# One attention layer on TensorE: bodies of 512 tokens against bodies of 1024, with q and k in 512-column matmuls

## The chip, the core and the metric

The kernel runs on one core of a Trainium2 chip. The metric is the device time of one execution in microseconds: the median of 3 runs of the kernel before is 1513.44 us (1513.13 to 1513.64). The core's engines are named as the profile names them: PE (TensorE matmuls), PEld (its weight loads), DVE (VectorE), ACT (ScalarE), POOL (GpSimd) and SP (SyncE, which here only issues DMAs).

## What is computed

```
x: (2048, 64, 128) f32; W_query, W_key, W_value, W_res: (128, 128) f32; HEADS, ATT_D = 4, 32
q, k, v = heads(x @ W_query), heads(x @ W_key), heads(x @ W_value)    # each (head, 2048, 64, 32)
scores  = einsum('hbqd,hbkd->hbqk', q, k)                             # 64x64 per head and sequence
out     = softmax(scores, axis=-1) @ v                                # heads side by side again: 128 columns
y       = relu(out + x @ W_res)
```

2048 sequences of 64 tokens go through one attention layer of 4 heads, without scaling or mask. All is float32 at the borders. The projections are made from x and the weights split in two float32r parts each (hi and lo), as hi*hi + hi*lo + lo*hi, which is why each projection is three matmuls into one accumulation.

## The kernel before

A tile is 128 tokens, that is two sequences (`SEQS`) side by side. A body is `TILES` = 4 tiles, 512 tokens; there are N = 256 bodies. Every engine's program is written out by hand, with semaphores between the engines, in a function `step(i, n)` that works on several bodies at once, i and its neighbours. ACT, DVE, POOL and SP have all steps unrolled (`run`). PE has steps 0 to 3 and the last ones unrolled, and between them a loop whose lap is 4 steps (`run_looped`, `Fori(1, N // RING - 1)`: 62 laps).

What one body needs:

- DVE transposes x in 32x32 blocks and splits it (`split_x`: L349 x_t, L353 x_hi, L355 x_lo).
- PE projects q and k (`project_qk`, L196 to L198), half a body (256 tokens) a call: q into one half of the bank `ps_qk`, k into the other. ACT copies the bank into `qk` (L291).
- PE projects the values and the residual (`project_vr`, L209 to L211), half a body a call, into the bank `ps_vr`. ACT copies it into `vr` (L298). Each call waits until the copy before it has emptied its bank.
- PE forms the scores (`score`, L220), each head from 32 partitions, 32 calls a body, into columns 0 to 255 of the four banks of `ps_so`. DVE takes the row maximum (L364) and subtracts it (L369, `shifted`).
- PE transposes the shifted scores (`transpose_shifted`, L232), half a body a call, into the bank `ps_pt`; ACT takes the exponential into `probs_t` (L311).
- POOL spreads the values into block-diagonal form (L167, `v_diag`). PE multiplies probabilities and values (`weigh_values`, L241, 16 calls a body) into columns 256 and up (`O_AT`) of the same four banks of `ps_so`. A column of ones in the values gives the row sums.
- DVE takes the reciprocals of the sums and multiplies (L375, L379, `attn`), POOL adds the residual (L154, `y`), ACT clips at zero (L304), SP stores.

PE's order in step i is: scores of the first half of body i, values of body i-2, scores of the second half of body i, transposes of body i-1 (first half), q and k of body i+1 (first half), `project_vr` of body i (first half), then transposes, q and k, and `project_vr` of the second halves. The scores of body i wait for `shifted_ready` of body i-1 and `attn_ready` of body i-3, since all share the banks of `ps_so`. On the other engines the order is that of their `step` functions.

Each matmul in float32 with a tile of less than the whole array (L220, L241) leaves two records in the trace, so the 16 calls of one run of scores show as x32; L232 and the projections leave one record a call.

## Time and profile before

| | us |
|---|---|
| median of 3 runs | 1513.44 |
| profiled execution, whole | 1513.46 |
| its span, first to last instruction | 1511.7 |
| PE busy | 1493.1 |
| DVE busy | 1390.5 |
| ACT busy | 1044.5 |
| POOL busy | 872.2 |

The whole time of the profiled execution is 1.8 us over its span. A busy share counts an engine as busy while any of its instructions is under way. PE's matmuls overlap in its pipeline: each record is 0.2 to 0.3 us long, while the next one starts 0.007 to 0.12 us after it. For PE the distance from start to start is therefore what is to be read.

### The profile page before, as it was taken

The numbers are of one execution on the slowest core, as the hardware profiler recorded it, in microseconds if no ns is written. First come the engines' busy times: TensorE is split into PE (matmuls) and PEld (weight loads), VectorE is DVE, ScalarE is ACT, GpSimd is POOL, SyncE is SP. The second block draws the span as 40 slices with busy tenths as digits, with TensorE's granted clock in tenths as the row PEclk, the third lists the DMA queues.
The fourth block names the chain that finished last, engine by engine and source line by source line (L and its number), as shares of the span: only waits on it lengthen the run. The fifth ranks groups of instructions, "written<-read, shape, count | busy, mean of one in ns | idle before, by whom it ended". The sixth has DMA issues, their size and how long they took to land.

```text
span 1511.7 us, 77248 instructions
## 1 busy us (share of the span) xinstructions
PE 1493.1 (99%) x32768; PEld 1405.2 (93%) x32768; DVE 1390.5 (92%) x1793; ACT 1044.5 (69%) x1794; POOL 872.2 (58%) x1548
## 2 busy tenths in 40 slices
PE   7999999999999999999999999999999999999997
PEld 6999999999999999999999999999999999999997
DVE  6999999999999999999999999999999999999996
ACT  4677777777777777777777777777777777777775
POOL 3555555555555555555555555555555555555555
PEclk9999999999999999999999999999999999999999
DMA  3444444444444444444444444444444444444443
GB/s 59 98 85 96 85 96 86 96 86 95 86 96 85 96 85 96 85 96 85 96 86 96 86 96 85 96 86 95 86 96 85 96 85 96 85 96 85 96 86 77
DMA packets 677302, 135.36 MB, mean 90 GB/s; under 512 B 545888, under 2 KB 677216, under 8 KB 677216
## 3 DMA queue, kind: packets, MB, share of 16 engines
q1 hardware_dynamic: 675840, 134.30, 42.9%
q14 instruction: 74, 0.61, 0.1%
q10 hardware_dynamic: 1376, 0.26, 0.1%
q8 instruction: 12, 0.20, 0.1%
HBM read 67.37 MB, written 67.11 MB: 89 GB/s over the span
## 4 chain that ended last, share of the span: by engine, by line
PE 98%; issue 0%; POOL 0%; DVE 0%; ACTq 0%; DMA 0%; ACT 0%; POOLq 0%
PE ps_so L241 18%; PE ps_pt L232 17%; PE ps_so L220 14%; PE ps_qk L198 8%; PE ps_qk L196 8%; PE ps_vr L209 8%; PE ps_qk L197 8%; PE ps_vr L210 8%; PE ps_vr L211 8%; POOL y L154 0%; DMA w_raw<-in_L_rec_W_res_dram 0%; ACTq L334 0%; POOL v_diag L167 0%; DVE row_max L364 0%; ACTq L331 0%
## 5 line engine op out<-in xcount | busy, mean ns | idle before, releaser
L154 POOL TENSOR_TENSOR y<-attn,vr 128x256 f32<-128x256 f32 x512 | 387.4, 779 | 532.4 <-DVE attn L379 512.7
L167 POOL COPY v_diag<-vr 64x264 f32<-64x264 f32 x1024 | 478.7, 467 | 102.9 <-POOL y L154 39.9
L311 ACT ACTIVATE probs_t<-ps_pt 128x512 f32<-128x512 f32 x512 | 307.0, 600 | 160.2 <-PE ps_pt L232 160.1
L364 DVE TENSOR_REDUCE row_max<-ps_so 128x16 f32<-128x1024 f32 x256 | 313.5, 1225 | 69.7 <-PE ps_so L220 69.7
L298 ACT COPY vr<-ps_vr 128x512 f32<-128x512 f32 x512 | 300.6, 587 | 67.3 <-PE ps_vr L211 1.1
L196 PE MATMUL ps_qk<-x_hi,w_hi 128*128 128x256 f32 x1024 | 331.3, 323 | 10.5 <-DVE x_lo L355 9.7
L291 ACT COPY qk<-ps_qk 128x512 f32<-128x512 f32 x512 | 300.6, 587 | 56.6 <-PE ps_qk L198 9.0
L232 PE MATMUL ps_pt<-ident,shifted 128*128 128x128 f32 x2048 | 321.4, 280 | 0.8 <-ACT probs_t L311 0.8
L369 DVE TENSOR_TENSOR shifted<-ps_so,row_max 128x1024 f32<-128x1024 f32 x256 | 313.5, 1224 | 8.8
L241 PE MATMUL ps_so<-v_diag,probs_t 128*64 128x66 f32 x8192 | 296.2, 225 | 1.4 <-DVE attn L379 0.7
L198 PE MATMUL ps_qk<-x_lo,w_hi 128*128 128x256 f32 x1024 | 292.0, 285 | 0.0
L209 PE MATMUL ps_vr<-w_hi,x_hi 128*128 128x256 f32 x1024 | 290.7, 284 | 0.0
L210 PE MATMUL ps_vr<-w_lo,x_hi 128*128 128x256 f32 x1024 | 290.2, 283 | 0.0
L197 PE MATMUL ps_qk<-x_hi,w_lo 128*128 128x256 f32 x1024 | 290.0, 283 | 0.0
L211 PE MATMUL ps_vr<-w_hi,x_lo 128*128 128x256 f32 x1024 | 289.0, 282 | 0.0
L304 ACT ACTIVATE y<-y 128x512 f32<-128x512 f32 x256 | 161.5, 631 | 175.2 <-POOL y L154 175.2
L241 PEld LDWEIGHTS ps_so<-v_diag,probs_t 128*64 128x64 f32 x8192 | 260.6, 137 | 19.0 <-ACT probs_t L311 0.9
L355 DVE TENSOR_TENSOR x_lo<-x_t,x_hi 128x512 fp32r<-128x512 f32 x256 | 269.3, 1052 | 8.8
L220 PE MATMUL ps_so<-qk 32*64 32x64 f32 x16384 | 249.8, 230 | 0.0
L232 PEld LDWEIGHTS ps_pt<-ident,shifted 128*128 128x128 f32 x2048 | 225.7, 141 | 18.4 <-ACT probs_t L311 1.2
L220 PEld LDWEIGHTS ps_so<-qk 32*64 32x64 f32 x16384 | 179.2, 132 | 51.8 <-issue 0.2
L196 PEld LDWEIGHTS ps_qk<-x_hi,w_hi 128*128 128x128 f32 x1024 | 196.7, 192 | 10.9 <-issue 9.7
(20 smaller groups left out, 1527.2 us busy)
## 6 DMA issues: line engine op xcount, KB each, us to landing
x_in<-in_r_x_dram SPq DMA_DIRECT2D x1024, 64.0 KB, 2.2
out_dram<-y SPq DMA_DIRECT2D x256, 256.0 KB, 2.5
w_raw<-in_L_rec_W_query_dram ACTq DMA_DIRECT2D x1, 64.0 KB, 2.2
w_raw<-in_L_rec_W_key_dram ACTq DMA_DIRECT2D x1, 64.0 KB, 2.7
w_raw<-in_L_rec_W_value_dram ACTq DMA_DIRECT2D x2, 32.0 KB, 2.7
w_raw<-in_L_rec_W_res_dram ACTq DMA_DIRECT2D x2, 32.0 KB, 2.7
```

The source lines that it names most:

```text
L154: nc.gpsimd.tensor_tensor(y[:, n % 2, a * HALF:(a + 1) * HALF].rearrange("k t (p j d) -> k j (t p) d", j=2, d=D), attn[:, n % 2, a * HALF: ...
L167: nc.gpsimd.tensor_copy(v_diag[n % 2][j * F:(j + 1) * F, seq, :, :, :, j].rearrange("k a t p d -> k a (t p) d"), vr[n][seq * F:(seq + 1) * ...
L196: nc.tensor.matmul(ps, w_hi[:, w, :], x_hi[n][:, tok], start=True, stop=False)
L197: nc.tensor.matmul(ps, w_lo[:, w, :], x_hi[n][:, tok], start=False, stop=False)
L198: last = nc.tensor.matmul(ps, w_hi[:, w, :], x_lo[n][:, tok], start=False, stop=True)
L209: nc.tensor.matmul(ps, x_hi[n][:, tok], w_vr_hi, start=True, stop=False)
L210: nc.tensor.matmul(ps, x_hi[n][:, tok], w_vr_lo, start=False, stop=False)
L211: last = nc.tensor.matmul(ps, x_lo[n][:, tok], w_vr_hi, start=False, stop=True)
L220: last = nc.tensor.matmul(ps_so[s * F:(s + 1) * F, at:at + F], qk[rows, a, 0, b * F:(b + 1) * F], qk[rows, a, 1, b * F:(b + 1) * F], start ...
L232: last = nc.tensor.transpose(ps_pt[:, c * P:(c + 1) * P], pair, ident[:, :])
L241: last = nc.tensor.matmul(ps_so[s * F:(s + 1) * F, at:at + 2 * VW], probs_t[:, a, t * PAIRS + p, s * F:(s + 1) * F], v_diag[n % 2][:, s, a ...
L364: nc.vector.reduce_max(row_max[:, :].rearrange("q (h u) -> q h u", h=HEADS), scores, AX_X).then_inc(max_ready, 1)
```

## The change

A body becomes 8 tiles, 1024 tokens, in four `GROUPS` of two tiles; N falls to 128 bodies and PE's loop to 30 laps of 4 steps. The scores of a body fill all 512 columns of the four banks of `ps_so` (head h in bank h); the results of its values take the same banks later (group a in bank a), after the shifted scores have been read out of them. So scores and values of all bodies alternate on the four banks: scores of body i, then values of body i-1, each in one run. The values wait for `shifted_ready` of body i, the scores for `attn_ready` of body i-2. `project_qk` makes q or k alone, 512 tokens a call, in three matmuls of 512 columns that fill the bank `ps_qk`. `ps_pt` becomes two banks in turn, `ps_vr` stays one. DVE makes `x_lo` behind the reciprocal and the multiplication, POOL moves values in two parts around the residual, the clip comes one step earlier, and the instructions of DVE, POOL (L154) and ACT (L304) are twice as wide. Parts that only rename or widen are left out here:

```diff
-TILES = 4
+TILES = 8
 HALF = 2
+GROUPS = TILES // HALF
-HTOK = HALF * P
+GTOK = HALF * P
+QTOK = BANK
 VW = D + 1
-O_AT = TILES * F
...
-        qk = sb("qk", [P, 2, 2, HTOK])
-
-        vr = [sb(f"vr{n}", [P, 2, 4, HALF, PAIRS, VW]) for n in range(RING)]
-
-        v_diag = [sb(f"v_diag{n}", [P, SEQS, 2, HALF, PAIRS, 2, VW]) for n in range(2)]
+        qk = sb("qk", [P, 2, TOK])
+
+        vr = [sb(f"vr{n}", [P, 4, GROUPS, HALF, PAIRS, VW]) for n in range(RING)]
+        v_diag = [sb(f"v_diag{n}", [P, SEQS, GROUPS, HALF, PAIRS, 2, VW]) for n in range(2)]
-        probs_t = sb("probs_t", [P, 2, HALF * PAIRS, P])
+        probs_t = sb("probs_t", [P, GROUPS, HALF * PAIRS, P])
-        ps_qk, ps_vr, ps_pt = banks("ps_qk"), banks("ps_vr"), banks("ps_pt")
+        ps_qk, ps_vr = banks("ps_qk"), banks("ps_vr")
+        ps_pt = [banks(f"ps_pt{n}") for n in range(2)]
...
+                if m + g > 0 or has(i - 1):
+                    pe.wait_ge(qk_ready, upto(i, m * 2 + g) - 1)
+                tok = slice(g * QTOK, (g + 1) * QTOK)
+                nc.tensor.matmul(ps_qk[:, :], w_hi[:, m, :], x_hi[n][:, tok], start=True, stop=False)
+                nc.tensor.matmul(ps_qk[:, :], w_lo[:, m, :], x_hi[n][:, tok], start=False, stop=False)
+                nc.tensor.matmul(ps_qk[:, :], w_hi[:, m, :], x_lo[n][:, tok], start=False,
+                                 stop=True).then_inc(qk_done, 1)
...
-                    pe.wait_ge(vr_ready, halves(i, a) - 1)
+                if a > 0 or has(i - 1):
+                    pe.wait_ge(vr_ready, upto(i, a) - 1)
...
-            def score(i, a):
-                for u in range(a * HALF, (a + 1) * HALF):
+            def score(i):
+                for u in range(TILES):
                     for s in range(SEQS):
                         for h in range(HEADS):
-                            b = u % HALF * SEQS + s
                             rows, at = slice(h * D, (h + 1) * D), h * BANK + u * F
-                            last = nc.tensor.matmul(
-                                ps_so[s * F:(s + 1) * F, at:at + F], qk[rows, a, 0, b * F:(b + 1) * F],
-                                qk[rows, a, 1, b * F:(b + 1) * F], start=True, stop=True)
-                return last
+                            tok = slice((u * SEQS + s) * F, (u * SEQS + s + 1) * F)
+                            last = nc.tensor.matmul(ps_so[s * F:(s + 1) * F, at:at + F], qk[rows, 0, tok],
+                                                    qk[rows, 1, tok], start=True, stop=True)
+                last.then_inc(s_done, 1)
...
-                if a == 1 or has(i - 1):
-                    pe.wait_ge(pt_ready, halves(i, a) - 1)
+                if a >= 2 or has(i - 1):
+                    pe.wait_ge(pt_ready, upto(i, a) - 2)
...
-                        last = nc.tensor.transpose(ps_pt[:, c * P:(c + 1) * P], pair, ident[:, :])
+                        last = nc.tensor.transpose(ps_pt[a % 2][:, c * P:(c + 1) * P], pair, ident[:, :])
...
-                for a in range(2):
+                for a in range(GROUPS):
...
-                                at = (a * HALF + t) * BANK + O_AT + p * 2 * VW
+                                at = a * BANK + (t * PAIRS + p) * 2 * VW
...
             def step(i, n):
                 if has(i):
+                    if has(i - 2):
+                        pe.wait_ge(attn_ready, i - 1)
                     if has(i - 1):
                         pe.wait_ge(shifted_ready, i)
-                    if has(i - 3):
-                        pe.wait_ge(attn_ready, i - 2)
-                    pe.wait_ge(qk_ready, halves(i, 0))
-                    score(i, 0)
-                if has(i - 2):
-                    pe.wait_ge(pt_ready, halves(i - 2, 1))
-                    pe.wait_ge(v_moved, (i - 2) * 4 + 4)
-                    if not has(i):
-                        pe.wait_ge(shifted_ready, N)
-                        pe.wait_ge(attn_ready, i - 2)
-                    weigh_values(i - 2, n)
-                if has(i):
-                    pe.wait_ge(qk_ready, halves(i, 1))
-                    score(i, 1).then_inc(s_done, 1)
-                if has(i - 1):
-                    pe.wait_ge(shifted_ready, i)
+                    pe.wait_ge(qk_ready, upto(i, 3))
+                    score(i)
+                else:
+                    pe.wait_ge(shifted_ready, N)
+                    pe.wait_ge(attn_ready, i - 1)
+                if has(i - 1):
                     transpose_shifted(i - 1, n + 1, 0)
                 if has(i + 1):
-                    project_qk(i + 1, (n + 1) % RING, 0)
+                    project_qk(i + 1, (n + 1) % RING, 0, 0)
+                if has(i - 1):
+                    transpose_shifted(i - 1, n + 1, 1)
                 if has(i):
                     project_vr(i, n, 0)
                 if has(i - 1):
-                    transpose_shifted(i - 1, n + 1, 1)
-                if has(i + 1):
-                    project_qk(i + 1, (n + 1) % RING, 1)
+                    transpose_shifted(i - 1, n + 1, 2)
+                if has(i + 1):
+                    project_qk(i + 1, (n + 1) % RING, 0, 1)
+                if has(i - 1):
+                    transpose_shifted(i - 1, n + 1, 3)
                 if has(i):
                     project_vr(i, n, 1)
+                if has(i + 1):
+                    project_qk(i + 1, (n + 1) % RING, 1, 0)
+                if has(i - 1):
+                    pe.wait_ge(v_moved, (i - 1) * 8 + 8)
+                    if has(i):
+                        pe.wait_ge(shifted_ready, i + 1)
+                    pe.wait_ge(pt_ready, upto(i - 1, 3))
+                    weigh_values(i - 1, n + 1)
+                if has(i + 1):
+                    project_qk(i + 1, (n + 1) % RING, 1, 1)
+                if has(i):
+                    project_vr(i, n, 2)
+                    project_vr(i, n, 3)
...
-                act.wait_ge(qk_done, halves(i, a))
+            def copy_qk(i, m, g):
+                act.wait_ge(qk_done, upto(i, m * 2 + g))
...
-                nc.scalar.copy(qk[:, a].rearrange("p w t -> p (w t)"), ps_qk[:, :]).then_inc(qk_ready, 1)
+                nc.scalar.copy(qk[:, m, g * QTOK:(g + 1) * QTOK], ps_qk[:, :]).then_inc(qk_ready, 1)
...
             def step(i, n):
-                if has(i - 3):
-                    clip(i - 3, (n + 1) % 2)
                 if has(i - 1):
                     exp_pt(i - 1, 0)
                 if has(i + 1):
-                    copy_qk(i + 1, 0)
+                    copy_qk(i + 1, 0, 0)
+                if has(i - 1):
+                    exp_pt(i - 1, 1)
                 if has(i):
                     copy_vr(i, n, 0)
                 if has(i - 1):
-                    exp_pt(i - 1, 1)
-                if has(i + 1):
-                    copy_qk(i + 1, 1)
+                    exp_pt(i - 1, 2)
+                if has(i + 1):
+                    copy_qk(i + 1, 0, 1)
+                if has(i - 1):
+                    exp_pt(i - 1, 3)
                 if has(i):
                     copy_vr(i, n, 1)
+                if has(i + 1):
+                    copy_qk(i + 1, 1, 0)
+                if has(i - 2):
+                    clip(i - 2, n)
+                if has(i + 1):
+                    copy_qk(i + 1, 1, 1)
+                if has(i):
+                    copy_vr(i, n, 2)
+                    copy_vr(i, n, 3)
...
-            def split_x(i, n):
+            def transpose_x(i, n):
...
+
+            def rest_of_x(i, n):
                 dve.wait_ge(xhi_ready, i + 1)
                 nc.vector.tensor_tensor(x_lo[n][:, :], x_t[:, :], x_hi[n][:, :].bitcast(F32),
                                         ALU.subtract).then_inc(xlo_ready, 1)
...
+                if has(i):
+                    shift_scores(i, n)
                 if has(i + 2):
-                    split_x(i + 2, (n + 2) % RING)
+                    transpose_x(i + 2, (n + 2) % RING)
+                if has(i - 1):
+                    normalize(i - 1, n + 1)
+                if has(i + 2):
+                    rest_of_x(i + 2, (n + 2) % RING)
```

The order on PE, first around the scores. Before, two runs of scores (`ps_so<-qk`) with the values (`ps_so<-v_diag`) between them, then the transposes (`ps_pt`):

```order
L220 MATMUL ps_so<-qk 64x64 x16
L241 MATMUL ps_so<-v_diag,probs_t 64x66 x16
L220 MATMUL ps_so<-qk 64x64 x16
L232 MATMUL ps_pt<-ident,shifted 128x128 x4
L196 MATMUL ps_qk<-x_hi,w_hi 128x256
```

And in the changed kernel, where line numbers are its own:

```order
L225 MATMUL ps_so<-qk 64x64 x64
L236 MATMUL ps_pt<-ident,shifted 128x128 x4
L201 MATMUL ps_qk<-x_hi,w_hi 128x512
L202 MATMUL ps_qk<-x_hi,w_lo 128x512
L203 MATMUL ps_qk<-x_lo,w_hi 128x512
L236 MATMUL ps_pt<-ident,shifted 128x128 x4
```

The scores of 8 tiles stand in one row of 64 calls, and the values have moved out from between them, to stand behind the third block of q and k.

The order on PE at the end of a step, with what each instruction waits for. Before, the second `project_vr` stands behind q and k, and its predecessor on the same bank is a whole group of q, k and transposes away:

```order
L232 MATMUL ps_pt<-ident,shifted 128x128 x3
L196 MATMUL ps_qk<-x_hi,w_hi 128x256 [waits qk_ready,xlo_ready]
L197 MATMUL ps_qk<-x_hi,w_lo 128x256
L198 MATMUL ps_qk<-x_lo,w_hi 128x256
L196 MATMUL ps_qk<-x_hi,w_hi 128x256
L197 MATMUL ps_qk<-x_hi,w_lo 128x256
L198 MATMUL ps_qk<-x_lo,w_hi 128x256
L209 MATMUL ps_vr<-w_hi,x_hi 128x256 [waits vr_ready]
```

And in the changed kernel, the third and the fourth `project_vr` of a body (the start of each is the row with a wait):

```order
L214 MATMUL ps_vr<-w_hi,x_hi 128x256 [waits vr_ready]
L215 MATMUL ps_vr<-w_lo,x_hi 128x256
L216 MATMUL ps_vr<-w_hi,x_lo 128x256
L214 MATMUL ps_vr<-w_hi,x_hi 128x256
L215 MATMUL ps_vr<-w_lo,x_hi 128x256
L216 MATMUL ps_vr<-w_hi,x_lo 128x256
L214 MATMUL ps_vr<-w_hi,x_hi 128x256 [waits vr_ready]
L215 MATMUL ps_vr<-w_lo,x_hi 128x256
```

The fourth `project_vr` stands right behind the third, on the same bank, with nothing between them.

## Rows read from the trace of the kernel before

**Rows 1.** Page, part 1: busy time, share of the span, instructions

```profile
span 1511.7 us, 77248 instructions
PE 1493.1 (99%) x32768; PEld 1405.2 (93%) x32768; DVE 1390.5 (92%) x1793; ACT 1044.5 (69%) x1794; POOL 872.2 (58%) x1548
```

**Rows 2.** Windows view, first values product to the last laps: busy, PEclk, DMA share, GB/s

```profile
24.80:1500.80 1476.00, 1475.27 (x32480) 1389.27 (x32469) 1376.11 (x1773) 1032.95 (x1776) 858.88 (x1523) 1.00 0.43 90
```

**Rows 3.** Timeline of a steady body: start us, us, engine, line, tiles, shapes, count

```profile
803.05 0.28 PE L210 MATMUL ps_vr<-w_lo,x_hi 128*128 128x256 f32 x1
803.17 0.28 PE L211 MATMUL ps_vr<-w_hi,x_lo 128*128 128x256 f32 x1
803.38 0.49 PE L220 MATMUL ps_so<-qk 32*64 32x64 f32 x32
803.79 1.16 PE L241 MATMUL ps_so<-v_diag,probs_t 128*64 128x66 f32 x32
804.88 0.49 PE L220 MATMUL ps_so<-qk 32*64 32x64 f32 x32
805.30 0.66 PE L232 MATMUL ps_pt<-ident,shifted 128*128 128x128 f32 x4
805.49 1.23 DVE L364 TENSOR_REDUCE row_max<-ps_so 128x16 f32<-128x1024 f32 x1 [0.25 <-PE ps_so L220]
805.71 0.36 PE L196 MATMUL ps_qk<-x_hi,w_hi 128*128 128x256 f32 x1
805.91 0.28 PE L197 MATMUL ps_qk<-x_hi,w_lo 128*128 128x256 f32 x1
807.23 0.60 PE L232 MATMUL ps_pt<-ident,shifted 128*128 128x128 f32 x4
807.58 0.36 PE L196 MATMUL ps_qk<-x_hi,w_hi 128*128 128x256 f32 x1
807.78 0.28 PE L197 MATMUL ps_qk<-x_hi,w_lo 128*128 128x256 f32 x1
809.19 0.49 PE L220 MATMUL ps_so<-qk 32*64 32x64 f32 x32
```

**Rows 4.** One line's view (L220), same body: duration ns min/median/max, first and last start

```profile
L220 PE MATMUL ps_so<-qk x64: 217/217/266, 803.4 to 805.2; 32*64 32x64 f32 x64
```

**Rows 5.** Timeline at the start of the execution, PE

```profile
12.16 0.55 PE L196 MATMUL ps_qk<-x_hi,w_hi 128*128 128x256 f32 x1 [0.83 <-ACT qk L291]
12.72 0.41 PE L198 MATMUL ps_qk<-x_lo,w_hi 128*128 128x256 f32 x1
12.93 0.41 PE L196 MATMUL ps_qk<-x_hi,w_hi 128*128 128x256 f32 x1
19.66 0.91 PE L220 MATMUL ps_so<-qk 32*64 32x64 f32 x64
```

**Rows 6.** Timeline at the end of the execution: a PE matmul that waited for ACT

```profile
1498.50 0.58 ACT L298 COPY vr<-ps_vr 128x512 f32<-128x512 f32 x1
1499.13 0.39 PE L209 MATMUL ps_vr<-w_hi,x_hi 128*128 128x256 f32 x1
1499.36 0.28 PE L210 MATMUL ps_vr<-w_lo,x_hi 128*128 128x256 f32 x1
1499.83 0.28 PE L211 MATMUL ps_vr<-w_hi,x_lo 128*128 128x256 f32 x1
1500.15 0.58 ACT L298 COPY vr<-ps_vr 128x512 f32<-128x512 f32 x1 [0.42 <-PE ps_vr L211]
```

**Rows 7.** Groups by line: count, busy us, mean ns, idle before and releaser

```profile
L167 POOL COPY v_diag<-vr 64x264 f32<-64x264 f32 x1024 | 478.7, 467 | 102.9 <-POOL y L154 39.9 <-ACT vr L298 16.4 <-PE ps_so L241 0.2
L369 DVE TENSOR_TENSOR shifted<-ps_so,row_max 128x1024 f32<-128x1024 f32 x256 | 313.5, 1224 | 8.8
L379 DVE TENSOR_TENSOR attn<-ps_so,inv_sum 128x512 f32<-128x512 f32 x256 | 177.1, 692 | 8.8
L298 ACT COPY vr<-ps_vr 128x512 f32<-128x512 f32 x512 | 300.6, 587 | 67.3 <-PE ps_vr L211 1.1
```

**Rows 8.** Page, part 6: a load's time from issue to landing

```profile
x_in<-in_r_x_dram SPq DMA_DIRECT2D x1024, 64.0 KB, 2.2
```

More of the change, by code:

```diff
@@ L97, in run @@
         def run(step):
-            for i in range(N + 3):
+            for i in range(N + 2):
                 step(i, i % RING)
@@ L107, in run_looped @@
                     step(ring * RING + n, n)
-            for i in range(N - RING, N + 2):
+            for i in range(N - RING, N + 1):
                 step(i, i % RING)
@@ L113, in has, with upto @@
             return not isinstance(i, int) or 0 <= i < N
+        def upto(i, g):
+            return i * GROUPS + g + 1
         def halves(i, a):
@@ L338, in _ @@
             act.wait_ge(ones_ready, 1)
-            copy_qk(0, 0)
-            copy_qk(0, 1)
+            for m in range(2):
+                for g in range(2):
+                    copy_qk(0, m, g)
             run(step)
```

145 lines of the change are left out of this document (72 added, 73 removed).

## The prediction

> **What bounds the kernel now.** I read the busy times first: PE 1493.1 of 1511.7 us, DVE 92%, ACT 69%, POOL 58% [rows 1]. The windows view over the 1476 us in which the bodies repeat has PE busy for 1475.27 us [rows 2]: PE waits for nobody there, so the time is the sum of PE's own starts. That window also has all 61 lap ends of PE's loop in it, so jumping back costs PE nothing visible today. The timeline of one body says what the sum is made of, read from start to start [rows 3]. The body lasts from 803.38 to 809.19, 5.81 us, so 11.62 us for 8 tiles and 256 x 5.81 = 1487 us of the span; the other 24 us are the filling and the emptying of the pipeline. Within a body:
>
> - A projection matmul of 256 columns starts 0.12 after the one before (803.05, 803.17).
> - Into the scores it is 0.21 (803.17 to 803.38), so 0.09 extra.
> - A run of scores is 0.49 long and its last record takes 0.217 [rows 4]: 0.27 from first to last start. The next kind of matmul starts 0.41 or 0.42 after the run's first, so the switch costs 0.15.
> - Values: 1.16 less 0.22 is 0.94 from first to last start, again 0.15 to the scores (803.79 to 804.88).
> - Four transposes, up to where a q/k matmul would nominally start: 0.41 + 0.20 - 0.12 = 0.49 behind the scores, 0.35 + 0.20 - 0.12 = 0.43 elsewhere (807.23, 807.58, 807.78).
>
> The sum for one body is 0.09 + 0.27 + 0.15 + 0.94 + 0.15 + 0.27 + 0.15 + 0.49 + 0.43 + 24 x 0.12 = 5.82, which is the body.
>
> **The change on PE.** The same sum for 8 tiles in the new order:
>
> Scores, one run of 64 calls, 128 records. Were it only four of the old runs it would take 4 x 0.27 = 1.08. But the trace has one run of 64 records, in a step without values: 0.91 long against 0.49 for 32 [rows 5, 3]. The second 32 records cost 0.42 where the first cost 0.27. I read this as PE having some 32 matmuls in hand when a run starts and being fed more slowly than it computes behind them; scores are the shortest matmuls, so they show it. At that pace the run takes 0.27 + 3 x 0.42 = 1.53. I take the middle, 1.30; the ends are 1.08 and 1.53.
>
> Values, one run: 2 x 0.94 = 1.88. Switches: 0.09 into the scores, 0.15 out of them, 0.09 into the values, and out of them 0.15 plus 0.10 for the slower first matmul of the full-array kind: 0.58 in all, against 2 x (0.09 + 0.15 + 0.15 + 0.15) = 1.08 today. Transposes: 0.49 + 3 x 0.43 = 1.78.
>
> q and k: 12 matmuls of 512 columns in place of 24 of 256. No row has such a width. The upper bound is 2 x 0.12 = 0.24 each. The lower bound comes from the start of the execution, where 256 columns take 0.21 (12.72 to 12.93) [rows 5]; at double that pace 512 columns take 0.21 too. In the steady body the 256 columns take 0.12 where half of 0.21 is 0.105, so part of the 0.12 is not columns. I take 0.22, nearer to the lower: 12 x 0.22 = 2.64, where 2.88 stood. [...]
>
> Values and residual projections: 24 x 0.12 = 2.88 as before, plus one **new wait**. The fourth `project_vr` stands right behind the third, on the one bank `ps_vr`, and waits until ACT has copied that bank. Today a group of transposes and q/k matmuls stands between any two. The tail shows the price part by part [rows 6]: the last matmul is 0.28 long, ACT starts 0.04 after its end (1499.83, 1500.15), copies for 0.59 [rows 7], PE starts 0.05 after that (1498.50 + 0.58 = 1499.08, then 1499.13), and its next start comes 0.23 later. Two starts thus take 0.28 + 0.04 + 0.59 + 0.05 + 0.23 = 1.19 where they take 0.24: 0.95 a body, or 122 us over the kernel. The wait for ACT after the first q/k block, 0.83 idle, is the same thing [rows 5]. ACT isn't late for it: its copy of q and k ends some 0.1 before the third `project_vr` does. Bounds: 0.68 if only the idle time counts, 0.95.
>
> Sum: 1.30 + 1.88 + 0.58 + 1.78 + 2.64 + 2.88 + 0.95 = 12.01 us a body. What the merged runs and the wide matmuls give back, 0.50 + 0.24, goes to the wait (0.95) and to the slower feeding (0.22).
>
> **The other engines.** DVE's instructions are twice as wide: 1024 elements take 1224 ns, 512 take 692 [rows 7], so 1.04 ns an element and 0.16 us fixed. Today's busy time for 8 tiles is 1390.5/128 = 10.9; seven fixed parts fewer make it 9.7 of 12.0. Its two waits on the path: from the last score to `shifted` is 0.12 + 2.29 + 0.03 + 2.29 = 4.7 us, and PE has transposes, three q/k blocks and two `project_vr` until the values, 0.15 + 1.78 + 1.98 + 1.44 = 5.3, so the wait on `shifted_ready` is covered with some 0.5 to spare. From the values to `attn` it is 1.6 us, covered by the last q/k block and 12 residual matmuls (3.3 with the new wait). POOL: 8 x 0.47 + 4 x 0.76 = 6.8 at most, and its moved values are due a whole body later. ACT: 12 x 0.59 + 1.3 = 8.4. A load of x becomes 128 KB, four a body; 64 KB land in 2.2 us [rows 8] and each is issued two bodies ahead; SP's stores are nowhere waited for within a body. These edits I cost at nothing; that cover is 0.5 us a body at its thinnest, on `shifted`.
>
> **Ends and laps.** 24 us of filling and emptying: both are counted in bodies, which double, though the fixed parts don't; between 24 and 40, I take 31. PE's loop: a lap today is 4 x 128 matmul records and as many loads, 1,024 instructions; after it is 4 x 244 x 2 = 1,952. The trace shows that 1,024 stay at hand over the jump [rows 2]; it doesn't show that 1,952 would. I take it that they don't, since the gap between these two is nearly a factor of two. A fetch is then a DMA, for which the nearest row is a load's 2.2 us [rows 8], less about 1.0 us of matmuls that PE has in hand: 1.2 x 29 jumps = 35 us. Bounds: 0, and 4.4 (two fetches in a row, nothing in hand) x 29 = 128. [...]
>
> The whole: 128 x 12.01 = 1537, + 31 + 35 = 1603 for the span, + 1.8 outside it = 1605 us. The profiled execution before is at the median of its runs (1513.46 and 1513.44), so nothing is to be added.
>
> **The rivals.**
> A, the lap is held: no fetch at the jump, 1570 us. For it: no jump costs anything today. Against it: the near doubling.
> B, the fetch is dearer, or the scores are fed at the slow pace throughout and lose what they have in hand at each jump: 1605 + 128 x 0.23 + 29 x 1.0 = 1663, up to 1700.
> C, faster. While PE waits for the bank at the end of the body, its instructions pile up in front of it, with their weights. Then the wait costs the idle 0.68 alone, the scores behind it run at 1.08, q/k at 0.213, and the lap is held: 12.01 - 0.27 - 0.22 - 0.08 = 11.44 us, 128 x 11.44 + 27 + 2 = 1493 us. It decides at 11.57 us a body: below that the kernel is faster. Against it: at the start of the execution the first matmul behind such a wait is the longest of all, 0.55 [rows 5], so its weights weren't there.
> D, the merged runs change nothing else and wait and gains cancel: a body of 11.6 us, 1513 us.
> E, DVE is slower on 2048 elements than its rate says and becomes the bound: over 12.3 us a body, 1610 and more. The wait would show on the values product.
>
> **How the numbers follow.** Mine 0.45, A 0.25, B 0.12, C 0.10, D 0.05, E 0.03. My case itself reaches from about 1575 to 1650 with the bounds of its terms. The range takes in A with its own bounds (1530 to 1600) and mine: 1525 to 1660; outside are C, D and B. Faster than by 0.2% is C and a little of D, 0.11; within 0.2% (about 3 us, what a measurement of this kernel tells from no change) 0.05; slower 0.84.
>
> **What would show it.** The timeline of one body: 12.0 us between runs of scores; the run of 128 records 1.3 + 0.22 long (1.08 + 0.22 would speak for A or C); 0.22 between the 512-column matmuls; about 0.65 us idle on the first matmul of every fourth `project_vr`, ended by ACT's copy of `vr`, 128 times; every fourth body about 1.2 us longer than the others if the laps are fetched, and all alike if they aren't. Wrong I am if that wait is missing, if PE is idle on the values product or on the scores, or if the body is under 11.6 us.

## The result, and the profile after

| | before | changed |
|---|---|---|
| median, us | 1513.29 (4 runs beside the changed kernel) | 1834.42 (1827.46 to 1841.17, 4 runs) |
| ratio to before, 95% interval | | 1.2122 (1.2076 to 1.2169) |
| profiled execution's span, us | 1511.7 | 1839.4 |
| mean granted clock of TensorE | 0.999 | 0.925 |

The change makes the kernel 21% slower. The forecast was 1605 us (1525 to 1660): slower, but 229 us too little. The page of the changed kernel, parts 1, 2, 3 and 5 (in part 5: busy us, mean ns of one, idle before and what ended it):

```profile
span 1839.4 us, 70912 instructions
PE 1568.5 (85%) x31232; PEld 1374.5 (75%) x31232; DVE 1173.5 (64%) x897; ACT 997.2 (54%) x1666; POOL 877.3 (48%) x1292
PEclk9999989899888999889998889898899889998899
...
q8 instruction: 313, 5.13, 1.2%
...
L389 DVE TENSOR_REDUCE row_max<-ps_so 128x32 f32<-128x2048 f32 x128 | 293.4, 2292 | 455.8 <-PE ps_so L225 455.8
...
L225 PE MATMUL ps_so<-qk 32*64 32x64 f32 x16384 | 234.8, 252 | 155.9 <-issue 155.2
```

PE was 99% busy before [rows 1] and is 85% now, and no other engine is near its own limit (DVE 64%, ACT 54%). PE's waits say what it waits for (line, total us, times, longest):

```profile
PE ps_so L225 <- issue: 155.2, 58, 4.7
PE ps_vr L214 <- ACT vr L312: 86.4, 128, 0.7
```

The second row is the foreseen wait for the bank: 128 times 0.68 us. The first isn't a wait for data. "issue" is idle time that nothing in the profile releases, 58 times, always on the scores. PE's loop has 30 laps and so 29 jumps back: two stalls a jump. The queue that carries instructions, q8, moved 5.13 MB in 313 packets. The same line of the page before:

```profile
q8 instruction: 12, 0.20, 0.1%
```

A packet is 16 KB. Such a packet is called a fetch below. And TensorE's granted clock, 1.00 all along before [rows 2], drops again and again.

A body that begins with a jump, on the timeline (start us, us, ..., idle before in brackets), and behind it a body without one:

```profile
747.52 0.28 PE L216 MATMUL ps_vr<-w_hi,x_lo 128*128 128x256 f32 x1
752.08 1.40 PE L225 MATMUL ps_so<-qk 32*64 32x64 f32 x68 [4.28 <-issue]
754.86 1.24 PE L225 MATMUL ps_so<-qk 32*64 32x64 f32 x60 [1.38 <-issue]
756.03 1.11 PE L236 MATMUL ps_pt<-ident,shifted 128*128 128x128 f32 x4
756.80 0.78 PE L201 MATMUL ps_qk<-x_hi,w_hi 128*128 128x512 f32 x1
757.37 0.63 PE L202 MATMUL ps_qk<-x_hi,w_lo 128*128 128x512 f32 x1
757.80 0.63 PE L203 MATMUL ps_qk<-x_lo,w_hi 128*128 128x512 f32 x1
...
768.42 1.59 PE L225 MATMUL ps_so<-qk 32*64 32x64 f32 x128
769.94 0.66 PE L236 MATMUL ps_pt<-ident,shifted 128*128 128x128 f32 x4
770.36 0.48 PE L201 MATMUL ps_qk<-x_hi,w_hi 128*128 128x512 f32 x1
770.67 0.39 PE L202 MATMUL ps_qk<-x_hi,w_lo 128*128 128x512 f32 x1
770.90 0.39 PE L203 MATMUL ps_qk<-x_lo,w_hi 128*128 128x512 f32 x1
...
775.36 2.09 PE L245 MATMUL ps_so<-v_diag,probs_t 128*64 128x66 f32 x64
777.38 0.50 PE L201 MATMUL ps_qk<-x_hi,w_hi 128*128 128x512 f32 x1
...
778.78 0.28 PE L216 MATMUL ps_vr<-w_hi,x_lo 128*128 128x256 f32 x1
779.74 0.39 PE L214 MATMUL ps_vr<-w_hi,x_hi 128*128 128x256 f32 x1 [0.68 <-ACT vr L312]
```

The same two stretches in the windows view (us, busy us by engine, granted clock, DMA share, GB/s):

```profile
747.80:768.42 20.62, 14.29 (x245) 12.46 (x245) 9.14 (x7) 7.85 (x13) 6.34 (x11) 0.75 0.34 77
768.42:780.65 12.23, 11.55 (x246) 10.18 (x245) 9.15 (x7) 7.75 (x13) 6.91 (x11) 1.00 0.28 45
```

The quiet body takes 12.23 us, close to the forecast's 12.01. The one with the jump takes 8.4 us more, in three pieces: 4.28 us of nothing at the jump, 1.38 us more after 68 of the 128 score records, and some 2.7 us because PE's work goes at half clock. The matmuls that follow start 0.43 apart, where in the quiet body it is 0.23. The granted clock is at 0.5 both in the scores behind the stall and in the matmuls behind them:

```profile
752.08:755.90 3.82, 2.44 (x128) 2.25 (x128) 0.00 (x0) 0.00 (x0) 0.00 (x0) 0.50 0.02 4
756.00:759.50 3.50, 3.50 (x17) 3.08 (x14) 3.33 (x2) 1.37 (x3) 0.00 (x0) 0.50 0.02 7
```

### The profile page after: what moved, and what is told of

Same layout as the page of the kernel before. It is cut to its first block and busy times, and to the rows that moved or that the text cites. A ratio compares the mean times of both kernels' runs of the same rounds, so it can differ in the third digit from the quotient of the medians.

```text
span 1839.4 us, 70912 instructions
## 1 busy us (share of the span) xinstructions
PE 1568.5 (85%) x31232; PEld 1374.5 (75%) x31232; DVE 1173.5 (64%) x897; ACT 997.2 (54%) x1666; POOL 877.3 (48%) x1292
## 3 DMA queue, kind: packets, MB, share of 16 engines
q8 instruction: 313, 5.13, 1.2%
## 5 line engine op out<-in xcount | busy, mean ns | idle before, releaser
L389 DVE TENSOR_REDUCE row_max<-ps_so 128x32 f32<-128x2048 f32 x128 | 293.4, 2292 | 455.8 <-PE ps_so L225 455.8
L151 POOL TENSOR_TENSOR y<-attn,vr 128x512 f32<-128x512 f32 x256 | 403.7, 1596 | 210.5 <-issue 207.5
L214 PE MATMUL ps_vr<-w_hi,x_hi 128*128 128x256 f32 x1024 | 330.2, 322 | 86.4 <-ACT vr L312 86.4
L394 DVE TENSOR_TENSOR shifted<-ps_so,row_max 128x2048 f32<-128x2048 f32 x128 | 293.3, 2291 | 4.4
L214 PEld LDWEIGHTS ps_vr<-w_hi,x_hi 128*128 128x128 f32 x1024 | 199.0, 194 | 119.0 <-ACT vr L312 112.8
L201 PE MATMUL ps_qk<-x_hi,w_hi 128*128 128x512 f32 x512 | 247.3, 483 | 16.8 <-DVE x_lo L383 13.7
L202 PE MATMUL ps_qk<-x_hi,w_lo 128*128 128x512 f32 x512 | 210.2, 411 | 0.0
L203 PE MATMUL ps_qk<-x_lo,w_hi 128*128 128x512 f32 x512 | 209.0, 408 | 0.0
L215 PEld LDWEIGHTS ps_vr<-w_lo,x_hi 128*128 128x128 f32 x1024 | 199.8, 195 | 6.0
L216 PEld LDWEIGHTS ps_vr<-w_hi,x_lo 128*128 128x128 f32 x1024 | 198.8, 194 | 0.0
```

What stands on the lines that cost most here:

```text
L151: nc.gpsimd.tensor_tensor(y[:, n % 2, tiles].rearrange("k u (p j d) -> k j (u p) d", j=2, d=D), attn[:, n % 2, tiles].rearrange("k u (p j) ...
L214: nc.tensor.matmul(ps, x_hi[n][:, tok], w_vr_hi, start=True, stop=False)
L215: nc.tensor.matmul(ps, x_hi[n][:, tok], w_vr_lo, start=False, stop=False)
L216: last = nc.tensor.matmul(ps, x_lo[n][:, tok], w_vr_hi, start=False, stop=True)
L389: nc.vector.reduce_max(row_max[:, :].rearrange("q (h u) -> q h u", h=HEADS), scores, AX_X).then_inc(max_ready, 1)
```

## Experiments

The kernel before, timed beside every run, was at 1513.1 to 1513.5 us. Every kernel here computes all of the layer.

**Theory and rival.** Theory: the jump costs it all, because the longer lap isn't held near PE and has to be fetched. Rival: the long runs of small matmuls, or the wait for the bank ahead of them, starve PE by themselves. A first pair takes the loop away, a second pair changes nothing but the loop of the kernel before.

### No loop on PE (e1_unrolled)

```diff
-            run_looped(pe, step)
+            for i in range(N + 1):
+                step(i, i % RING)
```

> The changed kernel with PE's steps written out one after another, no loop and no jump; everything else as it was. Theory (the jumps of PE's loop cost the time): the bodies that hold no jump in the changed kernel repeat every 12.23 us; 128 x 12.23 = 1565, and with some 30 us of filling and emptying about 1597 us in all, no idle on PE marked 'issue', granted clock at full speed throughout. Rival 1 (the instructions are fetched too slowly in any case, since a body's scores use them up faster than they come): idle moves from the jumps to the borders of the instruction blocks, over 1700 us. Rival 2 (the time is lost elsewhere and the jump only shows it): about 1834 us again.

Measured 1622.39 us (ratio 1.0725, 1.0707 to 1.0743). Its waits:

```profile
PE ps_vr L214 <- ACT vr L313: 86.3, 128, 0.7
PE ps_qk L201 <- DVE x_lo L384: 13.7, 1, 13.7
PE ps_pt L236 <- issue: 5.6, 4, 1.7
PE ps_so L225 <- issue: 3.3, 2, 1.8
```

Without a jump the 155 us on the scores are gone, the granted clock is 0.999, and the bodies are 12.23 us long. That is 212 us for the jumps, net of what the straight program loses itself. The time is 25 above what was expected. Some 15 of them are in ten bodies, about every 14th, that are 13.0 to 14.3 us long, so fetching straight on isn't free either; the profiled run was 4 us below the median, and the other 6 are in the ends.

### The kernel before with a lap of 8 steps (e2_before_lap8)

```diff
-            with engine.Fori(1, N // RING - 1) as ring:
-                for n in range(RING):
-                    step(ring * RING + n, n)
+            with engine.Fori(1, N // LAP - 1) as ring:
+                for n in range(LAP):
+                    step(ring * LAP + n, n % RING)
```

> The kernel before with one thing changed: a lap of PE's loop holds 8 steps in place of 4, so about 2,100 instructions in place of 1,059, and 30 laps in place of 62. The work and its order are the same. Theory (a lap that PE's instruction memory doesn't hold costs some 8 us at each jump): 1513 + 29 x 8.3 = 1755 us, with about 4 us idle on PE at each of 29 jumps, a lower granted clock behind it, and over 250 fetches of 16 KB on the instruction queue. Rival (the cost belongs to the new order or to the long runs of scores, not to the lap's length): 1513 us, as before.

Measured 1781.96 us, clock 0.938. Nothing of the change is in this kernel but the length of the lap (2,111 instructions between two jumps where 1,059 were), and it costs 269 us:

```profile
PE ps_so L221 <- issue: 178.6, 62, 3.9
```

Two stalls a lap here too, with short runs of scores. So the rival falls: no long run and no bank is needed.

### The kernel before without a loop (e3_before_unrolled)

The same edit as in the first run, in the kernel before.

> The kernel before with PE's steps written out one after another, no loop. It is the yardstick for the unrolled changed kernel. If a straight stream of instructions is fetched in time: 1513 us, the same as with the loop, with about 270 fetches of 16 KB. If the stream itself can't keep up: slower, by the idle time at the block borders (1 us at each of 270 would give 1780 us).

Measured 1562.05 us, 49 us more than with its loop, so the straight stream doesn't come in time here. The scores idle for issue 22 times, 22.1 us in all, and the other lines for 8 us; PE's busy time is 18 us longer too. A short lap that is held is better here than a straight program.

The trace has 66,820 instructions of PE, loads and sequencer's included, for 261 fetches, that of e1 63,236 for 247: 256 to a fetch. The 27 stalls for issue of over 0.5 us between 150 and 1411 us fit: each comes 193 or 194 instructions behind a multiple of 256. Such a stretch of 256 instructions is called a block below.

### The lap moved by idle waits (e4_lap_aligned)

```diff
+            for _ in range(310):
+                engine.wait_ge(ident_ready, 1)
```

> The changed kernel with 155 idle instructions (waits that are met already) in front of PE's loop, nothing else. In the profile the second stall of each lap always comes after 68 records of scores, which is some 139 instructions into the lap: a block border lies there. With 155 more instructions ahead the lap of 2,001 begins some 16 instructions into a block and ends at about 2,017, so it touches 8 blocks of 256, not 9. Theory A (8 blocks are held, the cost is that of the ninth): no stalls at the jumps, about 1597 us. Theory B (the block behind the lap's last one is fetched ahead and pushes the first one out): the first stall stays and the second one, at 68 records, moves or goes: 1700 to 1834 us.

The 310 waits are 155 instructions in the trace, as many as were meant. Measured 1933.73 us, 99 more than without the edit. In the records the borders between blocks are seen as gaps in the issue at instruction 241, 753 and 1,266 of the lap, counted from its first weight load, so the first block holds some 241 of its instructions and the lap does touch eight blocks (241 + 6 x 256 + 224); still there are 9 fetches a lap and the jump takes 3.4 to 4.5 us. Eight blocks alone don't hold it. Of the 99 us, 16 are one idle stretch ahead of the loop, where the waits stand. The others come with stalls at the new borders (47 us on the transposes, where none was), which now fall right ahead of, or at the end of, a run of scores; such a run uses up 256 instructions in 1.5 us.

### What the wait for the bank costs (e5_unrolled_reorder)

The unrolled kernel, with the third `project_vr` ahead of the fourth block of q and k, on PE and on ACT, so that no two of them stand next to each other:

```diff
                 weigh_values(i - 1, n + 1)
+                if has(i):
+                    project_vr(i, n, 2)
                 if has(i + 1):
                     project_qk(i + 1, (n + 1) % RING, 1, 1)
                 if has(i):
-                    project_vr(i, n, 2)
                     project_vr(i, n, 3)
```

> The unrolled changed kernel with one pair swapped on PE and on ACT: the third project_vr now stands ahead of the fourth q/k block, the fourth behind it, so that no two on the bank ps_vr follow each other. Theory (the wait for the bank costs about 0.95 us a body, of which 0.67 shows as idle): the idle on the first matmul of every fourth project_vr goes, a body falls from 12.23 to about 11.3 us, and the time from 1622 to about 1622 - 128 x 0.9 = 1507 us. Rival (DVE's chain behind the values is the next limit, since the swap puts nothing new there but shortens PE's way to the scores): a body of 11.6 to 12.0 us, PE idle on the scores for attn, 1545 to 1595 us.

Measured 1565.11 us (ratio 1.0348, 1.0309 to 1.0388), where 1507 was expected. PE's idle time for ACT is gone and the body is 11.51 us, 0.72 shorter, but 0.9 was expected. The wait isn't gone. It has moved under the q/k block that now stands between, and shows on the weight load of the fourth `project_vr` (PEld waits so 127 times, 52.4 us):

```profile
583.39 0.59 ACT L314 COPY vr<-ps_vr 128x512 f32<-128x512 f32 x1 [1.39 <-PE ps_vr L216]
...
583.66 0.39 PE L203 MATMUL ps_qk<-x_lo,w_hi 128*128 128x512 f32 x1
584.02 0.19 PEld L214 LDWEIGHTS ps_vr<-w_hi,x_hi 128*128 128x128 f32 x1 [0.41 <-ACT vr L314]
584.02 0.39 PE L214 MATMUL ps_vr<-w_hi,x_hi 128*128 128x256 f32 x1
...
584.25 0.28 PE L215 MATMUL ps_vr<-w_lo,x_hi 128*128 128x256 f32 x1
```

Two starts are 0.36 and 0.23 apart there, where 0.23 and 0.12 are usual: 0.24 of the 0.95 stay. Of the 128 x 0.72 = 92 us that the shorter bodies are worth, 57 came; PE's idle time for issue is 39 us here and was 13, and half clock 36 us where it was 6. The longest stalls are 2 to 2.9 us, about every 14th body.

### The width of q and k (e8_narrow_qk)

The kernel above, with q and k in 256-column matmuls as before:

```diff
-                nc.tensor.matmul(ps_qk[:, :], w_hi[:, m, :], x_hi[n][:, tok], start=True, stop=False)
+                for z in range(2):
+                    ps = ps_qk[:, z * GTOK:(z + 1) * GTOK]
...
+                    nc.tensor.matmul(ps, w_hi[:, m, :], x_hi[n][:, tok], start=True, stop=False)
```

> The unrolled kernel with the swapped order, and q and k in matmuls of 256 columns again, two for each of 512: 24 a body in place of 12. Theory (a 512-column matmul takes 0.233 us, two of 256 take 0.240): a body longer by 12 x 0.007 = 0.1 us, 10 to 15 us more than with 512 columns, plus what 24 more instructions a body do to the blocks. Rival (the wide matmuls hide weight loads of what stands around them and are worth more): a body longer by 0.3 us or more, 40 us and over.

Body 11.59 against 11.51 us: the wide matmuls bring 0.08 us a body, 10 us over the kernel. The time, 1583.96 us, is 19 above. 24 more instructions a body also mean more fetches (259 against 247), which may be the other 9; no run separates them.

### A hint on the jump (e6_hint, e7_hint_reorder)

```diff
-            with engine.Fori(1, N // RING - 1) as ring:
+            with nc.Fori(1, N // RING - 1, engines=[engine.engine], hint_back_edge=True) as ring:
```

> [...] Theory (the two stalls of a lap are late fetches of its first and second block, and the low clock behind them their consequence): the jump's 4 us and the 3.9 us idle behind it go; if the second block is then fetched in time too, nothing is left, 1597 to 1625 us; if only the first is helped, the idle at 68 records stays, 29 x 1.7 to 3 us, 1650 to 1700 us. Rival (the block is fetched only when the jump is taken, whatever is hinted): 1834 us.

Measured 1753.99 us: 80 less than the changed kernel, and above what was expected of either half of the theory. The jump itself falls from 4.1 to 0.45 us, and a lap has 9 fetches where it had 10: PE goes on before the next packet on q8 starts (1.2 to 3.1 us after the branch does), where without the hint it went on 1.3 to 1.5 us after that packet had ended. The second stall stays and grows (2.6 us in the median, at the 69th score record, where it was 1.6), and half clock behind it stays too. With the order of e5 too:

> The changed kernel with both: the hint in PE's loop and the swapped order of the third project_vr and the fourth q/k block. If both theories hold, the gains add: about 120 us less than with the hint alone, 1480 to 1510 us where the laps cost nothing, 1530 to 1590 us where a stall a lap stays. Rival (the wait for the bank gives the sequencer time, and without it the instructions run late more often): less than 80 us below the kernel with the hint alone.

Measured 1644.72 us (ratio 1.0872, 1.0854 to 1.0890). The reordering brings 109 us of the 120 expected, but the time misses the expected 1530 to 1590: bodies of 11.52, and 13.8 to 17.1 where the lap begins.

### The lap begun elsewhere (e9_lap_placed, e11_lap_placed2, e12_lap_placed3)

All three are e7 with the lap turned, and its first instruction placed in its block of 256 by an argument of the loop (`HEAD`). In e9 it begins with the transposes:

```diff
+            with nc.Fori(1, N // RING - 1, engines=[pe.engine], hint_back_edge=True,
+                         head_slot={pe.engine: HEAD}) as ring:
+                for n in range(RING):
+                    rest(ring * RING + n, n)
+                    scores(ring * RING + n + 1)
```

> The kernel with hint and swapped order, its lap turned and placed: PE's lap begins behind a run of scores (it is now the rest of step i, then the scores of i+1, four times), and its first instruction is loaded at slot 165 of a block of 256, so that the four score runs of a lap begin at slots 152 to 116. In the unrolled kernel the stalls come where a block border lies up to some 26 instructions ahead of a score run (the next one is then reached at records 115 to 127 of the run, 1.5 us later, and isn't there yet). Theory (a block is fetched when its forerunner is entered, and takes about 4 us to be there; only where 256 instructions are used up sooner does PE stand): no stalls but the jump's, a body of 11.51 us, 128 x 11.51 + 37 + 2 = 1512 us, up to 1530 with small ones left. Rival (each lap that isn't held costs its 4.5 us wherever it is cut): 1640 us as before the change of place.

Measured 1667.10 us (ratio 1.1014, 1.0997 to 1.1031), a miss. The stalls inside the lap are gone, but one of 3.7 us stands at the jump, in spite of the hint. The next one begins with the values, `HEAD` = 48 (`second` are the values and what follows them in a step, `first` what stands between scores and values):

```diff
+                for n in range(RING):
+                    second(ring * RING + n, n)
+                    scores(ring * RING + n + 1)
+                    first(ring * RING + n + 1, (n + 1) % RING)
```

> The reordered and hinted kernel again, with the lap turned once more: it now begins with the values, where the run before this one had it begin with the transposes. The first block of the lap then holds 208 instructions of it (values, third and fourth project_vr, fourth q/k block, 50 of the scores), some 4.9 us of work, and the last block is entered 208 instructions, some 6.2 us, ahead of the jump; the borders between fall at 50, 74, 98 and 122 instructions into the four runs of scores. Theory A (the engine resumes some 4 us after it enters the block before; the turned lap before this one failed only because its last block was entered 81 instructions of scores, some 0.5 us, ahead of the jump, so that the hint came too late): no stall at the jump nor inside the lap, the granted clock stays at 1, all bodies 11.52 us, 128 x 11.52 = 1475, and with 37 to 45 for the ends 1512 to 1522 us. Rival B (a jump outside what is held stalls PE for some 3.5 us wherever it stands, hint or not, unless it falls where PE is slow anyway): 3.8 us idle on the values at each of 30 laps and half clock behind it, about 1640 to 1670 us. Rival C (only the stall inside the lap stays): about 1580 us.

Measured 1636.8 us (ratio 1.0811, 1.0796 to 1.0826), a miss again, and by a slip of mine: the lap has 2,003 instructions, with the register ones, not 1,952, so that its last block began 3 instructions ahead of the jump. It touched nine blocks. The next one moves it by 24 slots and changes nothing else:

```diff
-HEAD = 48
+HEAD = 24
```

> The kernel of the run before this one with its lap moved by 24 instruction slots and nothing else. The trace of that run counts 2,003 instructions between two jumps, where its borders had been set out for 1,952: with 208 of them in the first block, the last block was entered 3 instructions ahead of the jump, not 208, and PE was idle for 2.7 to 3.3 us at each of 30 jumps. With 232 in the first block, the last one is entered 235 instructions ahead of the jump, and by the times of the matmuls in that trace every block of the lap holds 5.0 to 6.6 us of work. Theory A (PE resumes some 4 us after it enters the block before; a hinted jump costs nothing when the last block is entered early enough): no stall at the jump nor inside the lap, the granted clock stays at 1, all bodies 11.52 us, 128 x 11.52 = 1475, and with 37 to 45 for the ends 1512 to 1522 us. Rival B (a hinted jump costs some 3 us wherever it stands, or a lap whose start is placed in its block loses what the hint gives): 1625 to 1640 us, as the run before.

Measured **1513.83 us** (ratio 1.0008, 0.9999 to 1.0017). 123 us for 24 slots. Queue q8 and PE's waits, first e11:

```profile
q8 instruction: 284, 4.65, 1.1%
...
PE ps_so L246 <- POOL v_diag L167: 85.1, 29, 3.3
```

and then e12:

```profile
q8 instruction: 23, 0.38, 0.1%
...
PE ps_so L246 <- issue: 2.6, 1, 2.6
```

In e11 the view puts the stall at the jump down to POOL, whose record happened to end in it. It isn't POOL's: the branch itself takes 3.3 to 3.9 us there, and in e12, with the same order on every engine, both the stall and POOL's line are gone.

The time is the one expected, but not for the reason given. I had expected fetches that come in time; there are none: no fetch stands inside the loop, and the jump takes 0.22 us, as it did in the kernel before (0.21). The lap is **held**. It touches eight blocks (232 + 6 x 256 + 235).

### Which of the two holds it (e13_no_hint, e14_placed_hint)

e4 touched eight blocks without a hint and wasn't held; e6, e9 and e11 had the hint and nine blocks. So e12 without its hint:

```diff
-            with nc.Fori(1, N // RING - 1, engines=[pe.engine], hint_back_edge=True,
+            with nc.Fori(1, N // RING - 1, engines=[pe.engine],
```

> The held kernel of the run before (lap begins with the values, first block holds 232 of its instructions, eight blocks touched) without the hint on its jump; nothing else differs. Theory A (both are needed: without a hint PE also fetches the block that follows the last one of the lap in address order, which is a ninth and pushes the first one out): 9 fetches a lap, some 285 in all, a jump that holds PE for 3.5 to 4 us at each of 30 laps and half clock behind it: 1513 + 30 x (3.9 + 1.3) = about 1670 us, 1630 to 1700. Rival B (eight blocks are enough by themselves): 23 fetches, 1513 us.

Measured 1627.53 us, 9 fetches a lap, the jump 3.3 to 3.9 us:

```profile
q8 instruction: 284, 4.65, 1.1%
```

The lap is lost again, though the time stays a little below what was expected (a jump costs 113.7 / 29 = 3.9 us here, 2.9 of it idle, where 5.2 was expected). Both are needed in this order of work; for the changed kernel's own order e6 (hint alone, 1754), e4 (eight blocks alone, 1934) and the next run say the same. And the changed kernel in its own order, with hint and place and nothing else:

```diff
-            with engine.Fori(1, N // RING - 1) as ring:
+            with nc.Fori(1, N // RING - 1, engines=[engine.engine], hint_back_edge=True,
+                         head_slot={engine.engine: HEAD}) as ring:
```

> The changed kernel in its own order (the wait for ps_vr at the end of each body stays), its jump hinted and the start of its lap placed so that the first block holds 232 of its instructions and the last one 234: eight blocks. Theory A (the whole excess over the forecast's sum is the jump, and a lap of eight blocks with a hint is held): some 25 fetches in all, no idle for issue on the scores, every body 12.23 us, granted clock 1: 128 x 12.23 = 1565, and 37 to 42 for the ends and outside the span: 1602 to 1607 us, 230 us below the changed kernel. Rival B (what held the other kernel was its own order; here the scores at the very start of the lap still meet a missing block): 1754 us, as with the hint alone. Rival C (part of the excess has another cause): 1620 to 1700 us.

Measured **1614.26 us** (ratio 1.0670, 1.0655 to 1.0685), 220 us below the changed kernel. Its page and its waits:

```profile
span 1611.8 us, 70943 instructions
...
q8 instruction: 24, 0.39, 0.1%
```

```profile
PE ps_vr L216 <- ACT vr L314: 86.4, 128, 0.7
...
PE ps_so L227 <- issue: 5.7, 2, 3.2
```

122 of its bodies are 12.23 us long. The stalls that are left, two on the scores and one of 1.1 us on the transposes, are outside the held laps. Three bodies there are 16.6, 13.7 and 16.8 us long, 10 us more than they should be in all, which covers the 7 us by which it is over the expected 1607.

### The one part that gains, alone (e10_before_wide_qk)

The kernel before, with q and k of a whole body in 512-column matmuls. The scores then index one body's q and k, and all of them wait for the second block:

```diff
-                for w in range(2):
-                    ps = ps_qk[:, w * HTOK:(w + 1) * HTOK]
-                    nc.tensor.matmul(ps, w_hi[:, w, :], x_hi[n][:, tok], start=True, stop=False)
...
+                nc.tensor.matmul(ps_qk[:, :], w_hi[:, a, :], x_hi[n][:, :], start=True, stop=False)
...
```

> The kernel before with the wide matmuls alone: bodies of 512 tokens, the same order and the same lap of 4 steps, but project_qk makes q of the whole body in three matmuls of 512 columns at its first place and k at its second, in place of half a body of both. Theory (two matmuls of 256 columns take 0.240 us, one of 512 takes 0.233, and it saves 12 instructions a body, in a lap that is held): a body of 5.81 - 6 x 0.007 = 5.77 us, 1513 - 10 = about 1503 us. Rival 1 (the first 512-column matmul behind transposes starts its successor 0.32 us later, where 256 columns need 0.20, and eats the gain): 1513 us. Rival 2 (all scores now wait for the copy of k, which ends with the last project_vr, so PE waits up to 0.1 us a body): 1520 to 1540 us.

Measured 1511.30 us over 11 runs (ratio 0.9988, 0.9979 to 0.9997): 1.8 us less, a body of 5.80 for 5.81, where 10 were hoped for. The timeline shows why:

```profile
804.21 0.66 PE L228 MATMUL ps_pt<-ident,shifted 128*128 128x128 f32 x4
804.62 0.48 PE L193 MATMUL ps_qk<-x_hi,w_hi 128*128 128x512 f32 x1
804.94 0.39 PE L194 MATMUL ps_qk<-x_hi,w_lo 128*128 128x512 f32 x1
805.17 0.39 PE L195 MATMUL ps_qk<-x_lo,w_hi 128*128 128x512 f32 x1
805.40 0.28 PE L205 MATMUL ps_vr<-w_hi,x_hi 128*128 128x256 f32 x1
```

The second and third wide matmul bring 0.01 each (0.23 for 2 x 0.12); the first one behind the transposes takes 0.32, where two of 256 columns took 0.20 [rows 3] + 0.12 = 0.32. This is the fastest of all the versions, by 0.12%.

## Where the prediction was right and where it failed

The miss of 229 us, by the terms of the sum: the laps 230 us where 35 stood (+195), the steady body 0.22 x 128 (+28), the ends 39 where 33 stood (+6). The laps are the 220 us between e14 and the changed kernel and the 10 us that e14 loses in its three long bodies, which the changed kernel doesn't lose there. The ends are 1614.3 - 128 x 12.23 = 49, less the same 10.

- **What bounds the kernel, and the sum over PE's starts**: right. Every step of the sum can be read off the quiet body: scores to transposes 1.52 (1.45 forecast), values to the next start 2.02 (2.03), the start behind the bank's wait 0.96 after the one ahead of it and the next 0.22 later, with 0.68 idle (0.96, 0.23 and 0.65). Over the forecast is the stretch from the transposes to the values with the block of q and k behind them, 5.42 + 0.80 = 6.22 where the terms of the sum give 6.05 (1.78 + 2.64 + 12 x 0.12, and 0.19 of the switches around the values): 512 columns start 0.23 apart and not 0.22, and the second of three 0.31 to 0.34 behind the first.
- **The wait for the bank**: right in place, size, count and releaser. Moving one call takes 0.72 a body away, and the 0.24 that stay can be read off e5's timeline: 0.96 together, where 0.95 was forecast.
- **The cover of the other engines**: right. DVE's `row_max` and `shifted` take 2.29 us each, as worked out; nothing in the body waits for either.
- **The step that failed: the price of a jump.** I had said that the lap isn't held, which was right, and put 1.2 us on it: one fetch of 2.2 us, the time of a load [rows 8], less 1.0 in hand, with 4.4 as the utmost. It is 7.9 us on the mean of 29 jumps (230 / 29); of it 5.4 are idle (155 / 29), and the rest is work at half clock. Three things were wrong. A fetch isn't a load: PE stands for 3.7 to 5.1 us at each of the 29 branches (the next packet on q8 starts 1.0 to 2.8 us after the branch does, and PE goes on 1.3 to 1.5 us after that packet has ended). There is a second stall as well: the lap begins with the 256 instructions of the scores, used up in 1.5 us in a quiet body, and the second packet starts 3.0 to 4.3 us after the first; PE stands for 1.2 to 1.8 us more behind 68 score records. I read that as the second block coming late. And the granted clock falls to 0.5 at each jump, for 6.8 to 10.2 us, some of it while PE is still idle: 276 us of the changed kernel's execution are at half clock, 3.6 before. I had no term for that at all, in the sum or in the bounds, so even the range missed.
- **The lap itself.** That it isn't held the forecast argues from its near doubling. In blocks of 256 the changed kernel's lap touches nine; e14 has it in eight, with the hint, is held and costs 220 us less. The lap is 2,001 instructions in the trace, not the 1,952 of the sum, which left the register instructions out. Eight blocks were not enough without the hint (e13, e4: 9 fetches a lap), nor the hint with nine (e6, e7, e9, e11: 9 fetches a lap). The counts of fetches have a pattern: without the hint they are one more a lap than the blocks touched (10 for nine in the changed kernel, 9 for eight in e4 and e13), and with it as many (9 for nine in e6, e7, e9 and e11). So the hint spares one fetch a lap. Which block the spared one would have brought isn't shown, nor that it pushes out the first one, as theory B of e4 and theory A of e13 have it: the records don't name the block of a fetch.
- **The rivals.** A (the lap is held, 1570) is what e14 shows, at 1614. B had the right sign of the miss and a quarter of its size (58 of 229 us), with scores at 0.23 more a body, where they took 0.07 more. D fails with the body, 12.23 and not 11.6. C is refuted: scores behind the wait run no faster (1.52), and the wait costs 0.95 and not 0.68. E is refuted by DVE's rate.
- **What would show it**: "every fourth body about 1.2 us longer" was the line to read, and it said 8.4.

Left open: why the straight programs stall at some borders and not at others of the same place, and by how much the hint alone saves in a lap of more than nine blocks.

## What to carry to other kernels

Count the instructions of a hardware loop's lap, with loads and register instructions, before anything makes a body longer: where the lap stopped being held here, every jump cost PE a stall of some 4 us, a second one where the lap began with the scores, and mostly a stretch at half clock. The packets of the instruction queue say at once whether it is held (12 here against 313); a straight program has many too (247). The lap of 2,001 instructions was held with its start placed so that it touches eight blocks and a hint on its jump; both together were worth 220 us here, and then the kernel is decided by the things that the sum over starts had right.

## What the runs showed of the hardware that I had not expected

- A PE lap of 1,059 instructions was held; one of 2,001 to 2,003 was held only with the hint and when it touched eight blocks of 256 (23 and 24 fetches an execution against 284 to 313). A jump within what is held takes 0.21 us, outside 3.3 to 5.1, hinted 0.44 to 1.0 in e6 and e7, but 3.2 to 4.1 in e9 and e11. By the count of instructions the last block was entered some 70 instructions ahead of the jump in e6 and e7, that is 3.3 and 2.6 us in their traces; in e9 it was 120 instructions of scores, 0.6 us, and in e11 3 instructions. That this lead decides is argued, not shown: no run moves it alone.
- A straight instruction stream isn't free for PE: the kernel before loses 49 us unrolled (e3), at 261 fetches. In e1 and e5 stalls of 1.0 to 2.9 us come about every 14th body; that they stand at borders around runs in which 256 instructions pass in 1.5 us is a reading from counts (between 128 and 1518 us, e5's of over 0.5 us all come 193 to 195 instructions behind a multiple of 256).
- A long run of small matmuls slows down: the 128 score records take 1.38 us from first to last start, 10.8 ns each, where 32 take 0.27 [rows 3], 8.7 each. The forecast laid that on the feeding; no run tells it from the weight loads.
- At each of the changed kernel's 29 jumps, with 3.7 to 5.1 us at the branch and 1.2 to 1.8 more in the scores, the granted clock was 0.5 for 6.8 to 10.2 us, in which matmuls of 512 columns started 0.43 apart, not 0.23. In e11, with 2.7 to 3.3 us idle a jump and no second stall, 22 of 29 jumps brought it, for 3.4 us.
